# Mixture-of-experts, attention, mixture-of-experts on one core: some row tiles loaded transposed by DMA instead of turned by TensorE

## The reference

```python
def ffn(x, norm_w, gate_w, gate_b, w1, b1, w2, b2):      # both times with the same weights
    t = x * rsqrt(mean(x * x) + EPS) * norm_w
    logits = t @ gate_w.T + gate_b
    vals, idx = top_k(logits, 4)
    G = zeros((M, 16)).at[arange(M)[:, None], idx].set(softmax(vals))
    h = einsum('mh,eoh->emo', t, w1) + b1[:, None, :]
    a = minimum(h[..., ::2], LIMIT)
    b = clip(h[..., 1::2], -LIMIT, LIMIT)
    act = a * sigmoid(1.702 * a) * (b + 1.0)
    y = einsum('emi,edi->emd', act, w2) + b2[:, None, :]
    return x + einsum('me,emd->md', G, y)
x = x + 0.5 * ffn(layernorm(x), ...)
x = x + attention(layernorm(x), ...)                     # 16 heads of 16, causal, ALiBi
x = x + 0.5 * ffn(layernorm(x), ...)
```

## Time and profile before

| what | value |
|---|---|
| median of 3 runs | 904.75 us (904.38 to 905.96) |
| profiled execution, its own time | 903.41 us |
| its span, first to last instruction | 901.7 us |
| TensorE busy | 662.5 us, 73% of the span |
| VectorE, ScalarE, GpSimd busy | 72%, 57%, 40% |
| mean granted TensorE clock | 0.925 |
| HBM read, written | 79.13 MB, 64.24 MB |

### The profile page before, as it was taken

The page is one execution under the profiler, slowest core; times in us unless marked ns, Lnnn a source line. Parts: engine busy times, 40 slices in busy tenths (PEclk is TensorE's granted clock), DMA queues, the critical chain, the costliest instruction groups (busy, mean ns, idle before and its releaser), DMA issues.

```text
span 901.7 us, 22495 instructions
## 1 busy us (share of the span) xinstructions
PE 662.5 (73%) x5472; PEld 397.0 (44%) x5472; DVE 647.4 (72%) x2084; ACT 515.4 (57%) x1043; POOL 357.6 (40%) x513
## 2 busy tenths in 40 slices
PE   2222079999999917778898898886249999999920
PEld 2222046666666603223343353444126666666610
DVE  5888347777877765688687778648318888787757
ACT  2644058878888724257645636451048888888800
POOL 2777734444445414201200223335525444445420
PEclk9999999999999957899998999997569999999965
DMA  9866576666534363622301315439453333333158
GB/s 300 334 240 233 187 244 207 207 212 207 163 104 143 74 198 100 226 86 73 102 21 37 96 58 174 146 111 370 174 166 102 110 107 110 110 106 112 52 170 296
DMA packets 98930, 141.24 MB, mean 157 GB/s; under 512 B 16860, under 2 KB 78805, under 8 KB 98680
## 3 DMA queue, kind: packets, MB, share of 16 engines
q1 hardware_dynamic: 80472, 100.72, 35.2%
q0 software_dynamic: 13728, 34.64, 10.8%
q10 hardware_dynamic: 4608, 4.46, 1.4%
HBM read 79.13 MB, written 64.24 MB: 159 GB/s over the span
## 4 chain that ended last, share of the span: by engine, by line
PE 60%; DVE 12%; issue 9%; POOL 7%; ACT 5%; DMA 4%; ACTq 2%; SPq 0%; DVEq 0%; POOLq 0%
PE banks L457 23%; PE banks L477 11%; POOL x_rows L370 6%; PE banks L442 4%; PE banks L466 4%; ACT w2s L1574 3%; PE banks L1417 3%; PE banks L1375 2%; PE banks L1305 2%; PE banks L1351 2%; DVE pbh L1737 2%; DVE X L851 2%; PE banks L1328 2%; DVE X L1679 2%; DMA arena<-y_rows 1%
## 5 line engine op out<-in xcount | busy, mean ns | idle before, releaser
L390 POOL DMA_INDIRECT y_rows<-y,goal x158 | 156.1, 988 | 208.8 <-DVE y L817 107.5
L457 PE MATMUL banks<-w1s,rT 128*128 x948 | 234.0, 384 | 0.4 <-ACT rT L547 0.4
L1737 DVE CUSTOM_DVE_ANT_0 pbh<-banks,maskq 128x128 bf16<-128x128 f32 (+3 forms) x256 | 113.2, 487 | 40.7 <-PE banks L1328 33.1
L1574 ACT ACTIVATE w2s<-banks 128x1024 f32<-128x1024 f32 (+3 forms) x128 | 89.7, 701 | 88.5 <-PE banks L1359 86.1
L788 DVE TENSOR_SCALAR pbh<-banks 128x256 f32<-128x256 f32 x158 | 67.0, 424 | 93.9 <-ACT pbh L554 91.2
L477 PE MATMUL banks<-w2s,hsT 128*128 x948 | 129.5, 273 | 3.1 <-DVE hsT L810 3.1
L457 PEld LDWEIGHTS banks<-w1s,rT 128*128 128x128 f16 x948 | 86.7, 99 | 77.6 <-issue 4.5
L581 ACT ACTIVATE banks<-arena 128x512 f32 x158 | 95.0, 602 | 38.8 <-issue 24.7
L547 ACT ACTIVATE rT<-banks 128x512 f16<-128x512 f16 x158 | 93.7, 594 | 5.5 <-PE banks L442 4.5
L1267 POOL DMA_INDIRECT x_rows<-row,row_to x64 | 62.3, 974 | 85.6 <-PE banks L1359 49.5
L477 PEld LDWEIGHTS banks<-w2s,hsT 128*128 128x128 f16 x948 | 85.3, 98 | 12.4 <-issue 3.8
(11 more groups left out here) (251 smaller groups left out, 1057.9 us busy)
## 6 DMA issues: line engine op xcount, KB each, us to landing
row<-x_rows SPq DMA_DIRECT2D x158, 136.0 KB
arena<-in_w SPq DMA_DIRECT2D x16, 512.0 KB, 6.3
w1s<-y_rows SPq DMA_DIRECT2D x16, 512.0 KB, 5.0
arena<-y_rows SPq DMA_DIRECT2D x16, 512.0 KB, 8.0
arena<-b_rows SPq DMA_DIRECT2D x10, 768.0 KB, 10.7
qk_split<-w1s SPq DMA_DIRECT2D x48, 128.0 KB
arena<-qk_split SPq DMA_DIRECT2D x64, 96.0 KB, 2.5
w_lent<-w1s SPq DMA_DIRECT2D x22, 256.0 KB
```

The costliest lines, as they stand in the source:

```text
L390: pool.indirect_dma_start(y_rows[m], bass.IndirectOffsetOnAxis(ap=goal[:, n % NG, :], axis=0), y[:, n % NY, :], None, bounds_check=K * T - ...
L457: mm = pe.matmul(o, rT[:, n % 2, 2 * r + k, :], w1s[:, bass.ds(e, 1), k, w, :], start=False, stop=(k == HC - 1 and w == 1), skip_group_che ...
L1574: act.activation(probs[j][:, 2 * pl:2 * pl + 2, :], banks[:, 2:4, 0:SEQ - j * P], ACT.Exp, scale=0.25).then_inc(s("exp"), 1)
L1737: dve.tensor_tensor_reduce(junk[:, (n * U + j) % 3, 0:W], query_bank[(n * U + j) % 3][:, 0:W], maskq[:, SEQ - W:], 1.0, -3e38, ALU.add, AL ...
```

## The change

From the ninth slot of each layer on, a slot with an odd number is loaded otherwise (`by_load`): SP issues a transposing DMA of the 512 float16 columns straight into the tile's buffer, seen as 4 x 128, and a second, plain DMA of the 16 goal cells (64 bytes a row). TensorE doesn't turn such a slot, ScalarE doesn't copy it, and up reads its stationary operand from the row buffer in place of `rT`. These are slots 9, 11, ... 77 in layer 0 (35) and 87, 89, ... 157 in layer 1 (36), 71 in all. The other slots are loaded, turned and copied as before.

What follows from it: the buffer of such a slot is free only when up(n) has read it, so the load eight slots later waits for `up` and not for `turned`. The semaphore of a buffer counts 32 for such a slot. The PSUM banks 0 and 1 take turns by the count of turned slots (`turned_upto`), and the gate turns and bias products use the bank of the last turned slot (`side_bank`). The turn of gates waits for the last residual that read the bank.

```diff
+            rowsT = rows.rearrange("p c (q n) -> p c q n", q=4)
...
+            def by_load(n):
+                return n % SLOTS >= NX and n % 2 == 1
+
+            def turned_upto(n):
+                return sum(not by_load(i) for i in range(n + 1))
+
+            def loads_upto(n):
+                return sum(32 if by_load(i) else 16 for i in range(n % NX, n + 1, NX))
+
+            def turned_slot(t):
+                return [i for i in range(2 * SLOTS) if not by_load(i)][t - 1]
+
+            def side_bank(s):
+                return (turned_upto(s + 1) - 1) % 2
...
                 def load_rows(n, row0):
                     c = n % NX
+                    if n >= NX and by_load(n - NX):
+                        sp.wait_ge(each("up"), n - NX + 1)
+                    elif n >= NX:
+                        sp.wait_ge(each("turned"), turned_upto(n - NX))
                     if n >= NX:
-                        sp.wait_ge(each("turned"), n - NX + 1)
                         sp.wait_ge(each("goal"), n - NX + 1)
                     if m == 0 and n < E:
                         sp.wait_ge(padded[n // 4], 64)
-                    sp.dma_start(whole[:, c, :], x_rows[m][bass.ds(row0, P), :]).then_inc(loaded[c], 16)
+                    if by_load(n):
+                        sp.dma_start_transpose(rowsT[:, c], x_rows[m][bass.ds(row0, P), 0:H].bitcast(f16)).then_inc(loaded[c], 16)
+                        sp.dma_start(whole[:, c, H:], x_rows[m][bass.ds(row0, P), H:]).then_inc(loaded[c], 16)
+                    else:
+                        sp.dma_start(whole[:, c, :], x_rows[m][bass.ds(row0, P), :]).then_inc(loaded[c], 16)
...
                 def turn_rows(n):
-                    c = n % NX
-                    pe.wait_ge(loaded[c], 16 * (n // NX) + 16)
-                    if n >= 2:
-                        pe.wait_ge(each("rT"), n - 1)
-                    if gates_at(n - 3) is not None:
-                        pe.wait_ge(each("byT"), m * B + gates_at(n - 3) + 1)
-                    if bias_at(n - 3) is not None:
-                        pe.wait_ge(each("residual"), m * NT + bias_at(n - 3) + 1)
+                    c, t = n % NX, turned_upto(n)
+                    pe.wait_ge(loaded[c], loads_upto(n))
+                    if t > 2:
+                        pe.wait_ge(each("rT"), t - 2)
+                        for at in range(max(FIRST, turned_slot(t - 2) - 1), turned_slot(t - 1) - 1):
+                            if gates_at(at) is not None:
+                                pe.wait_ge(each("byT"), m * B + gates_at(at) + 1)
+                            if bias_at(at) is not None:
+                                pe.wait_ge(each("residual"), m * NT + bias_at(at) + 1)
                     for q in range(4):
-                        mm = pe.transpose(bank16[n % 2][:, q * P:(q + 1) * P], rows[:, c, q * P:(q + 1) * P],
+                        mm = pe.transpose(bank16[(t - 1) % 2][:, q * P:(q + 1) * P], rows[:, c, q * P:(q + 1) * P],
                                           ident16[:, :])
                     mm.then_inc(each("turned"), 1)
...
                 def up(n, e):
-                    pe.wait_ge(each("rT"), n + 1)
+                    if by_load(n):
+                        pe.wait_ge(loaded[n % NX], loads_upto(n))
+                        left = rowsT[:, n % NX]
+                    else:
+                        pe.wait_ge(each("rT"), turned_upto(n))
+                        left = rT[:, (turned_upto(n) - 1) % 2]
...
-                            mm = pe.matmul(o, rT[:, n % 2, 2 * r + k, :], w1s[:, bass.ds(e, 1), k, w, :], start=False,
+                            mm = pe.matmul(o, left[:, 2 * r + k, :], w1s[:, bass.ds(e, 1), k, w, :], start=False,
...
                 def turn_gates(s, g):
-                    pe.wait_ge(each("rT"), s + 2)
+                    pe.wait_ge(each("rT"), turned_upto(s + 1))
                     pe.wait_ge(each("by_expert"), m + 1)
+                    if g:
+                        pe.wait_ge(each("residual"), m * NT + g * TPB)
...
-                    if s + 2 < LAST:
+                    if s + 2 < LAST and not by_load(s + 2):
                         turn_rows(s + 2)
...
                 def rows_out(n):
-                    act.wait_ge(each("turned"), n + 1)
-                    if n >= 2:
-                        act.wait_ge(each("up"), n - 1)
-                    act.activation(rT[:, n % 2], bank16[n % 2][:, 0:512].rearrange("p (q n) -> p q n", q=4),
+                    t = turned_upto(n)
+                    act.wait_ge(each("turned"), t)
+                    if t > 2:
+                        act.wait_ge(each("up"), turned_slot(t - 2) + 1)
+                    act.activation(rT[:, (t - 1) % 2], bank16[(t - 1) % 2][:, 0:512].rearrange("p (q n) -> p q n", q=4),
                                    ACT.Copy).then_inc(each("rT"), 1)
...
                     if s + 2 < LAST:
-                        rows_out(s + 2)
+                        if not by_load(s + 2):
+                            rows_out(s + 2)
                         up_bias_in(s + 2, held[s + 2])
```

More of the change, by code:

```diff
@@ L376, in goals_of @@
                     e = pool.value_load(slot_tab[0:1, 1, n - FIRST:n - FIRST + 1], min_val=0, max_val=E - 1)
-                    pool.wait_ge(loaded[c], 16 * (n // NX) + 16)
+                    pool.wait_ge(loaded[c], loads_upto(n))
                     if n >= NG:
@@ L481, in turn_gates @@
                 def turn_gates(s, g):
-                    pe.wait_ge(each("rT"), s + 2)
+                    pe.wait_ge(each("rT"), turned_upto(s + 1))
                     pe.wait_ge(each("by_expert"), m + 1)
+                    if g:
+                        pe.wait_ge(each("residual"), m * NT + g * TPB)
                     for t in range(TPB):
-                        mm = pe.transpose(bank16[(s + 1) % 2][0:PARTS, t * P:(t + 1) * P], by_expert[:, g * TPB + t, :],
+                        mm = pe.transpose(bank16[side_bank(s)][0:PARTS, t * P:(t + 1) * P], by_expert[:, g * TPB + t, :],
                                           ident16[:, :])
@@ L489, in bias_product @@
                 def bias_product(s, i):
-                    pe.wait_ge(each("rT"), s + 2)
+                    pe.wait_ge(each("rT"), turned_upto(s + 1))
                     pe.wait_ge(each("byT"), m * B + i // TPB + 1)
-                    pe.matmul(bank[(s + 1) % 2][:, 0:H], byT[0:PARTS, i // TPB % 2, i % TPB * P:(i % TPB + 1) * P],
+                    pe.matmul(bank[side_bank(s)][:, 0:H], byT[0:PARTS, i // TPB % 2, i % TPB * P:(i % TPB + 1) * P],
                               b2_parts[0:PARTS, :], start=True, stop=True).then_inc(each("bias_made"), 1)
@@ L587, in byT_out @@
                         act.wait_ge(each("bias_made"), m * NT + (g - 1) * TPB)
-                    act.activation(byT[0:PARTS, g % 2, :], bank16[(s + 1) % 2][0:PARTS, 0:512], ACT.Copy).then_inc(each("byT"), 1)
+                    act.activation(byT[0:PARTS, g % 2, :], bank16[side_bank(s)][0:PARTS, 0:512], ACT.Copy).then_inc(each("byT"), 1)
                 split = 0 if m == 0 else E
@@ L838, in residual @@
                     dve.wait_ge(each("bias_made"), m * NT + i + 1)
-                    dve.scalar_tensor_tensor(X[:, i, :], X[:, i, :], grow[:, i:i + 1], bank[(s + 1) % 2][:, 0:H], ALU.mult,
+                    dve.scalar_tensor_tensor(X[:, i, :], X[:, i, :], grow[:, i:i + 1], bank[side_bank(s)][:, 0:H], ALU.mult,
                                              ALU.add).then_inc(each("residual"), 1)
```

## The result

The changed kernel takes 890.57 us (median of 4 runs, 889.84 to 890.80) against 904.79 us before (4 runs beside them): 14.2 us less, a ratio of 0.984 with an interval of 0.9825 to 0.9854. In a second comparison it was 890.49 against 904.72 us, 0.9837 (0.9815 to 0.9858). The prediction was 889.2 us.

A forecast was written before the change was run, and what follows sets the result against it. TensorE's issue time was taken to bound the slots: 71 slots x 0.22 us = 15.6 us off, nothing added, so 904.75 - 15.6 = 889.2 us. Range 885.5 to 901 us.

The forecast's parts named there:

- TensorE's 0.22 us a slot: Expert slots: four row turns cost TensorE 0.22 us, by starts 2.40 us apart against 2.18 without a turn.
- The sum: Whole kernel: 71 x 0.22 = 15.6 us off, nothing added, giving 889.2 us.
- the side products: Gate turns and bias products in the last turned slot's PSUM bank: no longer wait, nothing taken off.
- Another engine late next: Activation turn behind ScalarE and VectorE: 0.38 us to spare, nothing taken off; rival at 904.75 us, chance 0.04.
- SP's queue: SP's row loads: two plain issues take 0.67 of a pair's 4.57 us, 3.9 left, about 3.0 with stores.
- The forecast that all is hidden: Row loads: all latency of the transposed loads is hidden, with 11.1 us to spare for plain ones; only throughput could be late.
- The point from which the serial rival decides: Transposed load: the change loses to the kernel before from a price of about 3.5 us.
- the serial rival: A transposed load holds DMA engines or SP's queue for over 3.5 us; at 4.9 us, 1003 us; chance 0.11.
- the signs of being wrong: Profile after: TensorE idle for row DMA, issues of a microsecond and more, DMA share near 1, late scatters or activation turns.
- The transposed load's pieces: DMA engines: columns move in 256-byte pieces, taken at 0.5 us a load, plus 0.08 for goal cells.
- the dear rival: Transposed load in 32-byte pieces, 2.5 us each, late while weights are stored: 894 to 901 us, chance 0.08.
- the element-wise one: Transposed load falls apart into single elements, 39 us each: about 3400 us, chance 0.03.

The follow-up runs named there:

- the idle turns: Changed kernel plus four unread identity transposes on TensorE wherever a row turn fell away: layers 191.57 and 190.53 us, 938.52 against 938.96 us before, ratio 0.9994.
- ScalarE's copies: Changed kernel plus an unread same-size ScalarE copy wherever one fell away: layers 183.98 and 182.65 us, ratio to the kernel before 0.9876.

## Why the prediction was right, and where it wasn't

**TensorE's 0.22 us a slot: right, and shown.** Slots alternate between 2.40 and 2.17 us, the idle turns bring all of it back, ScalarE's copies none. The one slot of the old trace without a turn (2.18 us) held the whole forecast of TensorE's side in one row.

**The sum: 15.6 forecast for the slots.** The two traces of before and the two of the changed kernel give layer 0 191.47 and 191.04 against 183.38 and 183.86, 7.6 us by the means for 7.7; layer 1 190.21 and 190.20 against 183.03 and 182.97, 7.2 us for 7.9. Most of what is missing in layer 1 (0.6 of 0.7 us) lies in the four slots with the first bias product behind a turn of gates: 2.61 to 2.69 us from up to up, where they took 2.51. That product waits for ScalarE's copy of the turned gates; before, a row turn stood between the two. I had costed the side products at nothing.

**Another engine late next: right to take nothing.** With two of three slots loaded transposed, two slots in a row still follow each other by 2.17 us. The 11 further slots account for 2.4 of the 3.4 us by which layer 1 got shorter. 0.6 more came from the gate slots, where a row turn stands between again. The first two slots of the stage, which vary from execution to execution (5.2 to 5.8 us), took 0.7 less, and a few slots took a little more.

**SP's queue: the term that was mis-sized.** The step said that two plain issues take 0.67 us of a pair and 3.9 us are left. It read the rows of the issue alone. Each load also has a read of the table and register work in front of it, 0.77 us, which the old trace held too, and which doesn't show in a list of waits, since SP waits for nothing in it. A pair after the change takes 0.34 + 0.77 + 1.23 + 0.20 + 0.42 + 0.77 = 3.7 us of 4.57: 0.8 us are left, and 0.6 by the waits of layer 1 (24.1 us in 39 pairs), since some issues run longer. That is far from 3.9 less an issue. With two stores the trace after has pairs of 4.7 and 4.9 us, more than a pair has, where the step left about 3.0 us. Behind the stores, layer 0 has a few more DMAs on SP (padding rows and the first loads for attention), which the step left out.

That this costs nothing in the changed kernel is due to the eight buffers. They held a lead of 18 us, and the stretch with the stores brought it down to 9.1 and 7.8 us in the two traces, where 5 is too little. So 3 to 4 us of the 13 above that were left. The forecast that all is hidden came true, but not for the reason given, and in layer 0 it held with luck.

**The point from which the serial rival decides** was therefore wrong: I put it at 3.5 us for a transposed load, by the DMA engines. On SP's queue a second issue of 1.23 us, 2.5 in all, in layer 1 alone already gives the whole gain back. The mechanism of that rival was the right one to name; its resource is the issuing queue and its edge was at least 1 us nearer than I said. Of the signs of being wrong, issues of the transposed load of a microsecond and more did come, at 1.23 us, and the time was right all the same.

**The transposed load's pieces: near.** Its DMA queue takes 0.267 x 180 / 36 = 1.34 us of the 16 engines a pair, less 0.52 for the plain load, 0.8 us for the transposed columns and the goal cells, against 0.5 + 0.08. The packets in this window, 30626 for 36 pairs, are 850 a pair; a plain load made some 146 in the old trace, so a transposed one with its goal cells makes about 700. The trace after has 18432 packets of 256 bytes in this window, 36 x 512, and the second issue in layer 1 adds 544 packets each, 512 and some completions. So the columns go in 512 pieces of 256 bytes, which rules out the 4096 pieces of the dear rival and the element-wise one. The last piece has landed 2.1 to 3.0 us after the start of its issue, under the 5 us that were forecast. The Trainium skill's 1309 ns for a 128 x 128 block (VectorE: DVE Perf Modes, The three transpose paths), taken as a rate, falls: four blocks hold SP for 1.23 us and the engines for less. The Trainium skill's statement that transposing DMAs are as fast as regular ones (Advanced Engine Details and Errata, X-Bar Transpose (TRN2)) holds roughly for the engines, 0.7 against 0.5 us, and not for the issue, 1.23 against 0.33 us. The measurements decide.

**The median** fell by 14.2 us where the slots of two traces give 14.8. The difference is within the scatter of attention.

## What to carry to other kernels

A step moved to a DMA is paid on the queue that issues it: add up that queue's whole period, every issue, table read and register operation between two issues, and compare it with the period of the bound engine, before asking whether the DMA engines have room. A list of waits shows only how much of the queue's time is free, so read the drop of that figure: 90 us of waiting before, 24 after, and none in layer 0 was the sign that one step more would cost. Where a queue never waits, look at how far ahead of its use each load is issued: a lead that falls from slot to slot is a queue that is too slow, though nothing is late yet. And an irregular slot in the old trace, here the last one without a turn, can show the price of a change without building it.

## What was not expected of the hardware

- A transposing DMA of 128 x 512 float16 holds the issuing queue for 1.22 to 1.23 us (medians of 142 and 71 issues; one in ten runs longer, up to 2.4 us), the same in layer 0 at a DMA share of 0.71 and in layer 1 at 0.45; back to back, three take 3.83 us.
- The bytes that HBM was read for fell from 79.13 to 69.82 MB, though the same rows are loaded. The 9.31 MB are 71 x 131072 bytes, just the transposed columns, while the bytes on the DMA queues stay at 141.2 MB. With two issues in layer 1 the queues carry 4.7 MB more and the counter still says 69.82; with all slots loaded so it says 60.52. This counter doesn't see them. A lower figure of HBM reads is no saving here.
- Two executions of one program differ by 3 us in attention, and 1.7 of them lie in one group of 12 products, at a granted clock of 1.00 in one and 0.64 in the other.
